# Three attentions with heads of 8: twenty direct heads over six PSUM banks, and another form of the DMAs that build the stacks

## The chip, the cores and the metric

The kernel runs on one core of a Trainium2 chip (trn2). The metric is the time of one execution on the device in microseconds (us). TensorE is called PE, VectorE DVE, ScalarE ACT, GpSimd POOL, and SyncE, which only issues DMAs here, SP.

## The reference, cut to what matters

A decoder of four layers on `x` of 8 x 256 tokens x 128 features, all float32. Three of its twelve blocks are attentions with 16 heads of 8 features each: the one at the head of layer 1's hybrid block, layer 1's attention to the context, and layer 3's attention to the context. All three have this core (this is layer 3's, 8 batches of 256 queries and 256 keys):

```
q = (query @ Wq.T + bq).reshape(b, tq, 16, 8).transpose(0, 2, 1, 3)
k = (key @ Wk.T + bk).reshape(b, tk, 16, 8).transpose(0, 2, 1, 3)
v = (value @ Wv.T + bv).reshape(b, tk, 16, 8).transpose(0, 2, 1, 3)
scores = jnp.einsum('bhqd,bhkd->bhqk', q, k) / np.sqrt(8)
attn = jax.nn.softmax(scores, axis=-1)
out = jnp.einsum('bhqk,bhkd->bhqd', attn, v)
```

Layer 1's attention to the context has no projections of queries and keys. The rest of the decoder (wide attentions, gated and routed MLPs, a state-space block, scans) is not touched.

## The kernel before, in words

The program is one sequence of blocks. The class `Narrow` writes all three attentions; each has 8 x 16 = 128 heads, numbered g = 16 b + h, taken in pairs, one pair to a step p. The orders of PE, DVE and ACT are written out by hand in loops over p from -24 to 71.

A head is used twice. In **comparing** (`weigh_and_compare_pe`, the `compares` part) PE computes its scores with queries on the partitions (two halves of 128 x 256, one PSUM bank) and DVE reduces them to the negated maximum of each query (`maximum_dve`, L1256). When a batch's 16 maxima are there, `cut_maxima_dve` (L1271 to L1279) cuts them into three bf16 parts and PE transposes them (L1240, `neg`). In **weighing**, ten steps behind (`AHEAD = 10`), PE adds the maxima (selector products, `SEL`) and the scores the other way round, ACT takes the exponential (L1342), and PE sums the values (`sum_pe`). So comparing pair x = 2 (p + 10) stands in the same step as weighing pair p: x = 16 and 18 are compared at p = -2 and -1, and at p = 0 weighing begins beside the comparing of x = 20.

Scores must be exact to float32, but PE is fast only in bf16. So queries and keys are cut into three bf16 parts by POOL (`cut_pool`, L1403 to L1419; four steps a batch), and eight products of parts are stacked into 8 x 8 = 64 partitions for one head. The stacks are made through DRAM: `spread` (L1446) writes the parts to `parts`, and L1465 reads a batch's stack of 128 partitions x 2 x 4096 bytes, 1 MB, back. A write is 64 partitions x 3 (or 2) copies x 512 bytes, and a batch has 12 of them. All go out on SP's queue in `sync`, batch after batch, except the eight of batch 1's first two parts, which ACT issues in `act` after its masks. Per batch `sync` waits for the batch's writes (`parts_out`), then issues the read; from batch 3 on the read also waits until the buffer's old heads are scored (there are three stacks), which is at step p = 8 (b - 2) - 1. The batch is first needed at x = 16 b, which is p = 8 (b - 2) + 6.

Before the first stack is there, the first 16 heads (`DIRECT = 16`) are compared **directly** in float32: ACT makes a masked copy of the queries for each pair (L1382) and PE multiplies it with all keys, two heads of a pair on the two halves of the array's rows. Banks 4 and 5 hold the scores of one head each, alternately; before a head's products PE waits for the maximum of the head that had the bank (`maxed`). Banks 0 to 3 are those of weighing, 6 and 7 serve sums and all small work.

```
        direct = x < self.DIRECT
        if compares and (x == self.DIRECT or x % H == 0 and not direct):
            pe.wait_ge(*s.loaded_stack(x // H % 3).at(x // H))
```

Of the kernel before, what the change touches and what calls it, by code (L numbers as in the profile page):

```python
# [10 lines left out]
AXX = mybir.AxisListType.X  # L11


B, S, D = 8, 256, 128
P = 128
# [3 lines left out]
H = 16  # L19
HD = D // H  # L20
HW = 64
# [259 lines left out]
def table_act(k, act, func):  # L281

    k.tables += 1
    act.activation(k.small[:, k.tables:k.tables + 1], k.small[:, 0:1], func)
# [183 lines left out]
def mm(pe, out, lhsT, rhs, start=True, stop=True):  # L468
    return pe.matmul(out, lhsT, rhs, start=start, stop=stop, skip_group_check=True)  # L469
# [592 lines left out]
class Narrow:  # L1062
# [6 lines left out]


    AHEAD = 10
    DIRECT = 16
    FIRST = -24
    STEPS = B * H // 2
    LAST = STEPS + 8
# [41 lines left out]
    def masked(self, b, w):  # L1117
        if b == 0:
            return self.expo[w // 2][:, w % 2 * S:(w % 2 + 1) * S]
        return self.expo[7][:, w * S:(w + 1) * S] if w < 2 else self.accs[w - 2]  # L1120

    def other(self, p):

        r, i = divmod(p, H // 2)
        kind, b = (("project", r + 3), ("value", r + 1), ("turn 0", r - 1), ("turn 1", r - 1), (None, 0), ("back", r - 1),
                   ("neg", r + 1), ("out", r - 1))[i]
        there = kind is not None and 0 <= b < B
        if there and self.projection is None and kind in ("project", "value"):
            there = False
        return (kind, b) if there else None  # L1130
# [14 lines left out]
    def weigh_and_compare_pe(self, pe, p):  # L1145
        k, s = self.k, self.k.s
        weighs, compares = 0 <= p < self.STEPS, 0 <= p + self.AHEAD < self.STEPS
        a, x = 2 * p, 2 * (p + self.AHEAD)
        if weighs:
            b, h = divmod(a, H)  # L1150
            if h == 0:
                pe.wait_ge(*s.flip_s.at("neg", b))
            if a == 0:
                pe.wait_ge(*s.loaded_stack(0).at(0))
            for i in range(2):
                g, rows = a + i, slice(HW * i, HW * (i + 1))
                if g >= 4:
                    pe.wait_ge(*s.weighed.at("e", g - 4))
                mm(pe, k.bank[g % 4][:, :], k.SEL[rows, h + i, :], self.negt[b % 3][rows, :].unsqueeze(1).to_broadcast([HW, HALVES, S]), True, False)
# [3 lines that stand above are left out]
        if compares and direct:  # L1163
            pe.wait_ge(*s.lowered.at("masked", x // H, x % H // 2))
        for i in range(2):
            g, y = a + i, x + 1 - i
            if compares and y - 2 >= 0:
                pe.wait_ge(*s.maxed.at("x", y - 2))
            for c in range(HALVES):
                if weighs:  # L1170
                    m = mm(pe, k.bank[g % 4][:, c * S:(c + 1) * S], self.head(1, g)[:, c * P:(c + 1) * P], self.head(0, g), False, True)
                    if c:
                        m.then_inc(*s.scored.up("s", g))
                if compares:
                    queries, keys = self.head(0, y), self.head(1, y)
                    if direct:
                        rows = slice(HW * (y % 2), HW * (y % 2 + 1))
                        queries, keys = self.masked(y // H, y % H // 2)[rows, :], self.sources(y // H)[1][rows, :]
                    m = mm(pe, k.bank[4 + i][:, c * S:(c + 1) * S], queries[:, c * P:(c + 1) * P], keys)
                    if c:  # L1180
                        m.then_inc(*s.compared.up("x", y))

# [69 lines left out]
    def maximum_dve(self, dve, g):  # L1252
        s, (b, h) = self.k.s, divmod(g, H)
        neg = self.neg[b % 2].rearrange("p (t h) -> p t h", h=H)
        dve.wait_ge(*s.compared.at("x", g))
        dve.tensor_reduce(neg[:, :, h], self.k.bank[5 - g % 2][:, :].rearrange("p (t s) -> p t s", s=S), AXX, ALU.max,  # L1256
                          negate=True).then_inc(*s.maxed.up("x", g))

    def cut_maxima_dve(self, dve, b):
# [74 lines left out]
    def act(self, act):  # L1334
        k, s = self.k, self.k.s
        for p in range(self.FIRST, self.LAST):
# [12 lines left out]
            kind, b = self.other(p) or (None, 0)  # L1349
            if kind == "project":  # L1350
# [3 lines left out]
                if b == 3:  # L1354
                    act.wait_ge(*s.compared.at("x", self.DIRECT - 2))
                for n in range(2):
# [12 lines left out]
                act.activation(self.negt[b % 3], k.bank[7][:, :].bitcast(BF16)[:, 0:S], ACT.Copy).then_inc(*s.flip_s.up(kind, b))  # L1369
            if p in (self.FIRST, self.FIRST + H // 2):  # L1370
                self.mask_act(act, (p - self.FIRST) // (H // 2))
            if p == self.FIRST + H // 2:
                for c in range(2):
                    self.spread(act, 1, c)

    def mask_act(self, act, b):

        s, queries = self.k.s, self.sources(b)[0]
        if self.projection is not None:
            act.wait_ge(*s.stacked.at("project", b))  # L1380
        for w in range((min(self.DIRECT, (b + 1) * H) - b * H) // 2):
            act.activation(self.masked(b, w), queries, ACT.Identity, scale=self.k.w["same_d"][:, w:w + 1]).then_inc(*s.lowered.up("masked", b, w))  # L1382
# [53 lines left out]
    def spread(self, e, b, c):  # L1436

        s, dram, wide = self.k.s, self.k.parts_dram[b % 2], H // 2 * S
        e.wait_ge(*s.pool.at("cut", b, (0, 2, 3)[c]))
        for n, parts in enumerate((QUERY_PARTS, KEY_PARTS)):  # L1440
            among = [j for j in range(HD) if parts[j] == c]
            for o in range(2):
                row = n * P + o * HW + among[0] * HD
                place = bass.AP(dram.tensor, dram.offset + row * wide, [[S, HW], [(among[1] - among[0]) * HD * wide, len(among)], [1, S]])
                part = self.part(b, c)[o * HW:(o + 1) * HW, n * S:(n + 1) * S].unsqueeze(1).to_broadcast([HW, len(among), S])
                e.dma_start(place, part).then_inc(*s.parts_out[b % 2].up(*((b,) if (c, n, o) == (2, 1, 1) else (b, c, n, o))))  # L1446

    def sync(self, sp):


        k, s, wide = self.k, self.k.s, H // 2 * S
        for b in range(B):
            dram = k.parts_dram[b % 2]
            if b >= 2:
                sp.wait_ge(*s.loaded_stack((b - 2) % 3).at(b - 2))
            if b != 1:
                for c in range(3):
                    self.spread(sp, b, c)
            if b == 0:
                for c in range(2, 3):  # L1460
                    self.spread(sp, 1, c)
            if b >= 3:
                sp.wait_ge(*s.scored.at("s", (b - 2) * H - 1))
            sp.wait_ge(*s.parts_out[b % 2].at(b))
            sp.dma_start(self.stacks[b % 3].rearrange("p (n x) -> p n x", n=2),  # L1465
                         bass.AP(dram.tensor, dram.offset, [[wide, P], [P * wide, 2], [1, wide]])).then_inc(*s.loaded_stack(b % 3).up(b))


def raw_attention(k):
# [2957 lines left out]
```

## Time and profile before

| | us |
|---|---|
| median of 3 runs (2190.21 to 2195.07) | 2190.42 |
| the profiled execution, its own time | 2180.52 |
| its span in the profile | 2178.7 |
| first attention, first direct product to first weighing product | 348.25 to 372.06 |
| second attention, the same | 976.49 to 1004.24 |
| third attention, the same | 1904.35 to 1930.91 |

PE is busy for 87% of the span, DVE 70%, ACT 60%, POOL 27%. The profile is of one execution; times in its views count from the start of the span. An instruction's line is that of `kernel.py` before.

### The profile page before, as it was taken

Reading aid. Unit: us, or ns where it says so; the run is one execution under the profiler, and the core shown is the slowest. Engines: PE = TensorE matmul, PEld = TensorE weight load, DVE = VectorE, ACT = ScalarE, POOL = GpSimd, SP = SyncE. Lnnn points to the kernel's source line nnn. Section 1 sums busy time; section 2 is a strip of 40 time slices with the busy share of each in tenths; the row PEclk is TensorE's granted clock in tenths of the full one; section 3 lists DMA queues with packets and bytes.
Section 4 is the critical chain, followed back from the end, with each engine's and each line's share of the span. In section 5 each row is a group of like instructions: output and inputs, shape, how many; then the busy total and the mean of one; then the engine's idle time right before and its main releaser. Section 6 shows DMA issues by size and latency. Waiting matters only on the chain.

```text
span 2178.7 us, 37918 instructions
## 1 busy us (share of the span) xinstructions
PE 1892.0 (87%) x13392; PEld 1272.6 (58%) x13392; DVE 1522.0 (70%) x3631; ACT 1308.5 (60%) x2797; POOL 588.9 (27%) x569
## 2 busy tenths in 40 slices
PE   7999777997999999968987488999997997789896
PEld 5777565445777777644444255566665676544465
DVE  5777677865777677557847847989997457568553
ACT  5777533775878888734765746667665222347632
POOL 3223003102544443414101003344343001031035
PEclk9999897998999999977988699999999899889998
DMA  4000004411000000015402000000000100264022
GB/s 202 2 2 2 1 1 124 133 56 39 1 2 1 1 1 1 1 28 159 126 1 80 0 1 1 1 1 1 1 1 1 58 2 1 85 187 137 17 60 88
DMA packets 80155, 87.39 MB, mean 40 GB/s; under 512 B 6578, under 2 KB 70115, under 8 KB 79073
## 3 DMA queue, kind: packets, MB, share of 16 engines
q1 hardware_dynamic: 73633, 80.12, 11.6%
q10 hardware_dynamic: 4992, 2.36, 0.4%
q0 software_dynamic: 1344, 2.49, 0.4%
q8 instruction: 109, 1.79, 0.3%
q14 instruction: 77, 0.63, 0.1%
HBM read 54.39 MB, written 30.70 MB: 39 GB/s over the span
## 4 chain that ended last, share of the span: by engine, by line
PE 55%; DVE 28%; ACT 8%; issue 6%; POOL 2%; DMA 1%; ACTq 0%; DVEq 0%; POOLq 0%; SPq 0%
PE bank L469 46%; DVE scratch L1256 5%; PE bank L653 2%; ACT XN L2053 2%; PE bank L3010 2%; DVE scratch L3128 2%; DVE scratch L3148 2%; PE bank L368 2%; PE bank L693 1%; DVE XN L3168 1%; DVE stats L245 1%; DVE scratch L1665 1%; DVE w_keep L1952 1%; ACT L2131 1%; PE bank L1225 1%
## 5 line engine op out<-in xcount | busy, mean ns | idle before, releaser
L469 PE MATMUL bank<-scratch 64*128 64x256 bf16 (+5 forms) x2960 | 314.5, 303 | 22.2 <-DVE scratch L1256 13.3
L1256 DVE TENSOR_REDUCE scratch<-bank 128x2 f32<-128x512 f32 x384 | 244.5, 686 | 66.9 <-PE bank L469 66.1
L469 PE MATMUL bank<-w_keep,scratch 128*128 128x128 f32 (+4 forms) x1760 | 244.4, 330 | 18.7 <-DVE scratch L1995 4.1
L469 PEld LDWEIGHTS bank<-scratch 64*128 64x128 bf16 (+3 forms) x2960 | 178.8, 123 | 130.7 <-DVE scratch L1256 50.6
L1342 ACT ACTIVATE w_keep<-bank 128x512 f32<-128x512 f32 x384 | 212.5, 597 | 53.1 <-PE bank L469 45.2
L469 PE MATMUL bank<-XNT,w_keep 128*128 128x256 f32 (+4 forms) x800 | 235.6, 434 | 6.2 <-POOL w_keep L2192 5.7
L469 PEld LDWEIGHTS bank<-w_keep,scratch 128*128 128x128 f32 (+3 forms) x1760 | 182.9, 185 | 83.4 <-issue 54.9
L469 PEld LDWEIGHTS bank<-XNT,w_keep 128*128 128x128 f32 x800 | 149.1, 196 | 56.9 <-issue 28.3
L469 PE MATMUL bank<-w_early,scratch 64*128 64x256 f32 (+3 forms) x1152 | 160.9, 342 | 17.6 <-ACT w_early L3228 8.7
L469 PE MATMUL bank<-w_keep 128*32 128x256 f32 (+2 forms) x1728 | 153.4, 394 | 19.3 <-ACT w_keep L1342 5.4
L469 PEld LDWEIGHTS bank<-w_early,scratch 64*128 64x128 f32 (+3 forms) x1152 | 117.1, 182 | 62.6 <-issue 21.7
L795 ACT ACTIVATE scratch<-bank,scratch 128x256 f32<-128x256 f32 x256 | 100.3, 475 | 54.9 <-DVE scratch L721 54.9
L469 PE MATMUL bank<-scratch,w_early 128*128 128x256 f32 (+2 forms) x416 | 122.3, 438 | 8.5 <-DVE scratch L2555 4.4
L3228 ACT ACTIVATE w_early<-bank,scratch 128x256 f32<-128x256 f32 x172 | 82.9, 562 | 72.6 <-DVE scratch L3132 72.6
L721 DVE TENSOR_REDUCE scratch<-bank 128x2 f32<-128x512 f32 x128 | 82.5, 686 | 61.7 <-PE bank L469 61.6
L469 PEld LDWEIGHTS bank<-w_keep 128*32 128x32 f32 (+2 forms) x1728 | 70.2, 121 | 88.0 <-issue 47.2
L469 PE MATMUL bank<-XNT,w_early 128*128 128x256 f32 (+1 forms) x384 | 115.4, 430 | 4.5 <-ACT XNT L383 1.6
L3337 POOL TENSOR_TENSOR w_early<-w_early,scratch 128x1024 f32<-128x1024 f32 x43 | 81.4, 1892 | 136.6 <-DVE scratch L3153 136.6
L368 PE MATMUL bank<-w_keep,XN 128*128 128x128 f32 x192 | 48.2, 426 | 79.0 <-DVE XN L318 76.1
L3128 DVE TENSOR_REDUCE scratch<-bank 128x2 f32<-128x512 f32 x128 | 87.5, 684 | 22.1 <-PE bank L469 22.1
L469 PEld LDWEIGHTS bank<-scratch,w_early 128*128 128x128 f32 x416 | 72.1, 199 | 47.9 <-issue 30.1
L1952 DVE SCALAR_TENSOR_TENSOR w_keep<-w_keep,w_early 128x256 f32<-128x256 f32 x192 | 98.5, 562 | 0.1
(460 smaller groups left out, 3843.3 us busy)
## 6 DMA issues: line engine op xcount, KB each, us to landing
scratch<-parts SPq DMA_DIRECT2D x24, 1024.0 KB, 5.0
parts<-scratch SPq DMA_DIRECT2D x168, 96.0 KB, 2.3
parts<-scratch SPq DMA_DIRECT2D x96, 64.0 KB, 2.1
w_early<-pack_l3f SPq DMA_DIRECT2D x1, 5206.0 KB, 17.3
parts<-scratch ACTq DMA_DIRECT2D x24, 96.0 KB, 2.9
w_keep<-pack_l2f SPq DMA_DIRECT2D x1, 2124.0 KB, 13.1
w_early<-pack_mamba SPq DMA_DIRECT2D x1, 2120.0 KB, 18.9
w_keep<-pack_l2x SPq DMA_DIRECT2D x1, 2049.0 KB, 8.5
```

Of the source, the lines that this page charges most:

```text
L368: t = pe.transpose(k.bank[q][:, j * P:(j + 1) * P], src(i), k.w["ident"])
L469: return pe.matmul(out, lhsT, rhs, start=start, stop=stop, skip_group_check=True)
L653: m = pe.transpose(self.k.bank[3 + o][:, c * S + t * P:c * S + (t + 1) * P], self.expo[g % 4][:, t * S + c * P:t * S + (c + 1) * P], self. ...
L721: dve.tensor_reduce(self.neg[g % 4], self.scores(g)[:, :].rearrange("p (t s) -> p t s", s=S), AXX, ALU.max, negate=True).then_inc(*s.maxed ...
L795: a = act.activation(self.expo[g % 4][:, t * S:(t + 1) * S], self.scores(g)[:, t * S:(t + 1) * S], ACT.Exp, bias=self.neg[g % 4][:, t:t + 1])
L1256: dve.tensor_reduce(neg[:, :, h], self.k.bank[5 - g % 2][:, :].rearrange("p (t s) -> p t s", s=S), AXX, ALU.max, negate=True).then_inc(*s. ...
L1342: act.activation(self.expo[g % 8], k.bank[g % 4][:, :], ACT.Exp, scale=HD ** -0.5).then_inc(*s.weighed.up("e", g))
L1952: o = dve.scalar_tensor_tensor(out=yv[:, j, :], in0=xv[:, j, tap:tap + S], scalar=scale, in1=yv[:, j, :], op0=ALU.mult, op1=ALU.add)
L2053: a = act.activation(self.by_head(self.early[u % 2])[:, t, h, :], self.upto, ACT.Copy, scale=a3[:, t, h:h + 1])
L3128: dve.tensor_reduce(neg, self.k.bank[o][:, :].rearrange("p (t s) -> p t s", s=S), AXX, ALU.max, negate=True).then_inc(*s.maxed.up("x", p, o))
L3228: a = act.activation(self.weights(p, o)[:, t * S:(t + 1) * S], self.k.bank[o][:, t * S:(t + 1) * S], ACT.Exp, bias=self.bias[p % 2][:, o * ...
L3337: pool.tensor_tensor(ex, ex, self.sums[p % 2].unsqueeze(2).to_broadcast([P, 2 * HALVES, S]), ALU.mult).then_inc(*s.pool.up("scaled", p))
```

## The change

Three things, in all three attentions.

- `DIRECT` goes from 16 to 20, so two more pairs (x = 16 and 18, of batch 1) are compared in float32 and the wait for stack 1 moves from x = 16 (p = -2) to x = 20 (p = 0). ACT makes two more masked copies.
- The scores of the first 16 heads go around six banks, 4, 5, 0, 1, 2, 3 (`compare_bank`), and PE waits for the maximum of the head six places before (`reused`) instead of two. From head 16 on it is banks 4 and 5 as before. For banks 0 to 3 PE also waits until they are emptied of the transposes ahead of the attention (`turned_at`).
- `spread` writes 128 features at once, six writes a batch instead of twelve, with another order of rows in `parts`; ACT issues none any more. SP's order at the start is now batch 0's six, batch 1's first two, stack 0's read, batch 1's other four, stack 1's read. A read is four DMAs of 64 partitions x 4096 bytes instead of one of 128 x 2 x 4096, and its address list in DRAM begins with a count of 8 (8 x 8 rows) instead of 128.

```
-    DIRECT = 16
+    DIRECT = 20
...
+    def compare_bank(self, y):
+        m = y ^ 1
+        return self.k.bank[(4, 5, 0, 1, 2, 3)[m % 6] if m < H else 4 + m % 2]
+    def reused(self, y):
+        m = y ^ 1
+        m -= 6 if m < H else 2
+        return m ^ 1
...
-            if compares and y - 2 >= 0:
-                pe.wait_ge(*s.maxed.at("x", y - 2))
+            if compares and self.reused(y) >= 0:
+                pe.wait_ge(*s.maxed.at("x", self.reused(y)))
+            if compares and 2 <= y ^ 1 < 6:
+                pe.wait_ge(*self.turned_at((y ^ 1) - 2))
...
-            if p == self.FIRST + H // 2:
-                for c in range(2):
-                    self.spread(act, 1, c)
...
-            for o in range(2):
-                row = n * P + o * HW + among[0] * HD
-                place = bass.AP(dram.tensor, dram.offset + row * wide, [[S, HW], [(among[1] - among[0]) * HD * wide, len(among)], [1, S]])
-                part = self.part(b, c)[o * HW:(o + 1) * HW, n * S:(n + 1) * S].unsqueeze(1).to_broadcast([HW, len(among), S])
-                e.dma_start(place, part).then_inc(*s.parts_out[b % 2].up(*((b,) if (c, n, o) == (2, 1, 1) else (b, c, n, o))))
+            place = bass.AP(dram.tensor, dram.offset + (n * P + among[0] * H) * wide, [[S, P], [(among[1] - among[0]) * H * wide, len(among)], [1, S]])
+            part = self.part(b, c)[:, n * S:(n + 1) * S].unsqueeze(1).to_broadcast([P, len(among), S])
+            e.dma_start(place, part).then_inc(*s.parts_out[b % 2].up(*((b,) if (c, n) == (2, 1) else (b, c, n))))
...
-            sp.dma_start(self.stacks[b % 3].rearrange("p (n x) -> p n x", n=2),
-                         bass.AP(dram.tensor, dram.offset, [[wide, P], [P * wide, 2], [1, wide]])).then_inc(*s.loaded_stack(b % 3).up(b))
+            for o in range(2):
+                for n in range(2):
+                    rows = bass.AP(dram.tensor, dram.offset + (n * P + o * HD) * wide, [[H * wide, HD], [wide, HD], [1, wide]])
+                    sp.dma_start(self.stacks[b % 3][o * HW:(o + 1) * HW, n * wide:(n + 1) * wide], rows).then_inc(
+                        *s.loaded_stack(b % 3).up(*((b,) if o and n else (b, o, n))))
```

On SP, at the start of the first attention, the order was this (a batch's stack is the `scratch<-parts` row, shapes are partitions x copies or halves x elements):

```order
L1446 DMA parts<-scratch 64x3x256 x8
L1446 DMA parts<-scratch 64x2x256 x8
L1465 DMA scratch<-parts 128x2x2048 x2
L1446 DMA parts<-scratch 64x3x256 x8
L1446 DMA parts<-scratch 64x2x256 x4
L1465 DMA scratch<-parts 128x2x2048
```

And now it is this:

```order
L1454 DMA parts<-scratch 128x3x256 x4
L1454 DMA parts<-scratch 128x2x256 x2
L1454 DMA parts<-scratch 128x3x256 x2
L1474 DMA scratch<-parts 64x1x2048 x4
L1454 DMA parts<-scratch 128x3x256 x2
L1454 DMA parts<-scratch 128x2x256 x2
L1474 DMA scratch<-parts 64x1x2048 x4
```

Stack 0's read moved ahead of four of batch 1's writes, stack 1's read stands behind them, and each read is now four DMAs.

On PE, from the thirteenth head of the first attention on (`w_keep` are the masked queries and the direct keys, `scratch` the stacks), the order was:

```order
L469 MATMUL bank4<-w_keep 128x256 x2
L469 MATMUL bank5<-w_keep 128x256 x2
L469 MATMUL bank4<-w_keep 128x256 x2
L469 MATMUL bank5<-w_keep 128x256 x2
L469 MATMUL bank4<-scratch 128x256 x2
L469 MATMUL bank5<-scratch 128x256 x2
L1240 MATMUL bank7<-IDB,scratch 128x128 x2
L469 MATMUL bank4<-scratch 128x256 x2
L469 MATMUL bank5<-scratch 128x256 x2
L469 MATMUL bank0<-scratch,SEL 128x512
```

And now:

```order
L469 MATMUL bank4<-w_keep 128x256 x2
L469 MATMUL bank5<-w_keep 128x256 x2
L469 MATMUL bank0<-w_keep 128x256 x2
L469 MATMUL bank1<-w_keep 128x256 x2
L469 MATMUL bank4<-scratch,w_keep 128x256 x2
L469 MATMUL bank5<-scratch,w_keep 128x256 x2
L1253 MATMUL bank7<-IDB,scratch 128x128 x2
L469 MATMUL bank4<-scratch,w_keep 128x256 x2
L469 MATMUL bank5<-scratch,w_keep 128x256 x2
L469 MATMUL bank0<-scratch,SEL 128x512
```

The places of the instructions are the same; the last four direct heads of batch 0 go to four banks instead of two, and the two pairs around the transposes (L1240, now L1253) are direct products in float32 instead of products of the stack.

## Rows read from the trace of the kernel before

**Rows 1.** The page, costliest groups: the reductions of comparing (count, busy us, mean ns)

```profile
L1256 DVE TENSOR_REDUCE scratch<-bank 128x2 f32<-128x512 f32 x384 | 244.5, 686 | 66.9 <-PE bank L469 66.1
```

**Rows 2.** Timeline, second attention: start us, us, engine line operation xcount [idle before <-releaser]

```profile
973.46 1.15 POOL L1419 TENSOR_TENSOR scratch<-scratch 128x512 bf16<-128x512 f32 x1
...
976.49 2.08 PE L469 MATMUL bank<-CT,w_keep 64*128 64x256 f32 x8 [2.69 <-ACT w_keep L1382]
...
991.09 2.58 PE L469 MATMUL bank<-CT,w_keep 64*128 64x256 f32 x8 [0.34 <-DVE scratch L1256]
...
994.01 2.58 PE L469 MATMUL bank<-CT,w_keep 64*128 64x256 f32 x8 [0.34 <-DVE scratch L1256]
...
1004.24 1.20 PE L469 MATMUL bank<-scratch 64*128 64x256 bf16 x8
...
1014.06 0.90 PE L469 MATMUL bank<-scratch 64*128 64x256 bf16 x8 [0.47 <-DVE scratch L1256]
```

**Rows 3.** Timeline, first attention

```profile
350.25 1.28 DVE L1256 TENSOR_REDUCE scratch<-bank 128x2 f32<-128x512 f32 x2
...
350.32 1.16 POOL L1419 TENSOR_TENSOR scratch<-w_keep,scratch 128x512 bf16<-128x512 f32 x1
...
368.60 0.71 PE L469 MATMUL bank<-scratch 64*128 64x256 bf16 x4 [0.52 <-DMA scratch<-parts]
...
372.06 1.20 PE L469 MATMUL bank<-scratch 64*128 64x256 bf16 x8
...
383.86 0.90 PE L469 MATMUL bank<-scratch 64*128 64x256 bf16 x8 [0.47 <-DVE scratch L1256]
...
385.37 3.72 DVE L1256 TENSOR_REDUCE scratch<-bank 128x2 f32<-128x512 f32 x6
```

**Rows 4.** Timeline, third attention

```profile
1915.12 0.71 PE L469 MATMUL bank<-w_keep,CT 128*128 128x128 f32 x4 [3.03 <-ACT scratch L1357]
...
1930.91 1.20 PE L469 MATMUL bank<-scratch 64*128 64x256 bf16 x8
```

**Rows 5.** Timeline of SP's queue: start us, us for all issues together, xcount

```profile
2.12 0.43 SPq L4212 DMA_DIRECT2D w_early<-pack_l  x1
...
359.37 2.02 SPq L1465 DMA_DIRECT2D scratch<-parts  x2
...
971.38 10.62 SPq L1446 DMA_DIRECT2D parts<-scratch  x16
...
1031.54 0.36 SPq L1465 DMA_DIRECT2D scratch<-parts  x1
...
1045.91 0.37 SPq L1465 DMA_DIRECT2D scratch<-parts  x1
...
1894.10 0.35 SPq L4272 DMA_DIRECT2D w_early<-pack_l3f  x1
...
1916.26 1.73 SPq L1465 DMA_DIRECT2D scratch<-parts  x2
```

**Rows 6.** The page, DMA issues: xcount, KB each, median us from issue to landing

```profile
scratch<-parts SPq DMA_DIRECT2D x24, 1024.0 KB, 5.0
parts<-scratch SPq DMA_DIRECT2D x168, 96.0 KB, 2.3
...
w_early<-pack_l3f SPq DMA_DIRECT2D x1, 5206.0 KB, 17.3
```

**Rows 7.** Windows: stretch, us, busy time (xcount) of each engine, PE clock, DMA share, GB/s

```profile
370.00:374.00 4.00, 3.71 (x18) 1.64 (x19) 3.70 (x7) 1.52 (x3) 0.00 (x0) 0.50 0.52 127
...
450.00:453.50 3.50, 3.50 (x46) 1.59 (x40) 3.29 (x8) 2.70 (x6) 0.00 (x0) 1.00 0.84 298
...
450.50:453.00 2.50, 2.50 (x34) 1.23 (x28) 2.30 (x4) 2.14 (x5) 0.00 (x0) 1.00 0.90 369
...
1700.00:1710.00 10.00, 10.00 (x24) 5.12 (x24) 5.33 (x15) 3.06 (x5) 0.00 (x0) 0.78 0.07 21
...
985.00:990.00 5.00, 4.41 (x15) 3.49 (x16) 1.99 (x4) 0.00 (x0) 5.00 (x5) 0.50 0.97 371
```

More of the change, by code:

```diff
@@ L1178, in weigh_and_compare_pe @@
                         queries, keys = self.masked(y // H, y % H // 2)[rows, :], self.sources(y // H)[1][rows, :]
-                    m = mm(pe, k.bank[4 + i][:, c * S:(c + 1) * S], queries[:, c * P:(c + 1) * P], keys)
+                    m = mm(pe, self.compare_bank(y)[:, c * S:(c + 1) * S], queries[:, c * P:(c + 1) * P], keys)
                     if c:
@@ L1255, in maximum_dve @@
         dve.wait_ge(*s.compared.at("x", g))
-        dve.tensor_reduce(neg[:, :, h], self.k.bank[5 - g % 2][:, :].rearrange("p (t s) -> p t s", s=S), AXX, ALU.max,
+        dve.tensor_reduce(neg[:, :, h], self.compare_bank(g)[:, :].rearrange("p (t s) -> p t s", s=S), AXX, ALU.max,
                           negate=True).then_inc(*s.maxed.up("x", g))
@@ L1455, in sync @@
                 sp.wait_ge(*s.loaded_stack((b - 2) % 3).at(b - 2))
-            if b != 1:
-                for c in range(3):
-                    self.spread(sp, b, c)
+            for c in range(b == 1, 3):
+                self.spread(sp, b, c)
             if b == 0:
-                for c in range(2, 3):
-                    self.spread(sp, 1, c)
+                self.spread(sp, 1, 0)
             if b >= 3:
```

## The prediction, made before the changed kernel had run

> **What bounds the kernel now.** I read the page first. PE is busy for most of the span, but the change touches 384 of DVE's reductions and the products before them, and of those reductions DVE stood idle 66.9 us in all, nearly all of it waiting for PE [rows 1]. So I looked at where that idle time lies. The timeline puts it at the three starts. In the second attention the direct pairs follow each other every 994.01 - 991.09 = 2.92 us [rows 2], while six reductions in a row take 3.72 us, 1.24 a pair [rows 3]: with two banks PE and DVE take turns. The bound of that start is this ping-pong: 27.75 us from the first direct product (976.49) to the first weighing product (1004.24) [rows 2], with PE at the lower of its two clock levels, 1.2 GHz (granted clock 0.50 [rows 7]).
>
> The first attention is different. Its pair x = 16 waited last for a DMA, the read of stack 1 at 368.60 [rows 3]. The DMA engines are close to full there. So two chains run side by side up to the first weighing: PE and DVE, and cut, write, read, cut, write, read. In the first attention the DMAs end last, in the second the compute. In the third, PE also stood 3.03 us because ACT, busy with issuing DMAs, emptied a bank late, until 1915.12 [rows 4]. After the start each batch takes 1045.91 - 1031.54 = 14.4 us [rows 5], and no read is waited for.
>
> **The compute chain, after.** With six banks a pair needs no turn of DVE's. The two heads run side by side as the first pair did: 2.08 us at the lower clock at 976.49 [rows 2]. Ten pairs then take at most 20.8 us, or, if the clock rises, 20 reductions of 0.62 = 12.4 us. Two more direct pairs are in that count; ACT's two more masks hide in its idle time. In the second attention this makes PE ready for weighing between 976.49 + 2.08 + 12.4 = 991 and 976.49 + 20.8 = 997.3, against 1004.2. In the first, DVE starts at 350.25 [rows 3]; 12.4 us, and an estimated 3.5 for the cut of the maxima and the projections in between, give 366, that is 18 us after its first product. In the third the same 18 us from 1904.35 give 1922, the stall of 3.03 us gone since ACT issues nothing.
>
> **The DMA chain, after.** PE's first weighing step now waits for stack 1, so this chain decides. Its terms:
>
> - Issue. Twelve-write batches cost 10.62 / 16 = 0.66 us a DMA [rows 5]. DMAs of 128 partitions cost 0.43, as at 2.12 [rows 5]. I take 0.45 for a write. A read's piece has 64 partitions, so 0.65: four take 2.6 us.
> - Writes' data. With only writes in flight, 127 GB/s at a DMA share of 0.52 [rows 7]: 1.05 MB takes 8.26 x 0.52 = 4.3 us of all 16 engines. Batch 1's last four writes are 10/16 of it, 2.7 us.
> - Reads' data. 1.05 MB at 298 GB/s and share 0.84 is 2.95 us of all engines, at 369 and 0.90 it is 2.56 [rows 7]; 2.75 in the middle. Issue to landing is 5.0 [rows 6].
> - How many engines a piece uses. From 1700 to 1710 one DMA was in flight, L4263, whose list begins with 127 rows: a DMA share of 0.07 and 21 GB/s [rows 7], one engine of sixteen. Lists that begin with 128 or 64 fill all of them. A count is shared out in equal parts or not at all, so I read a list that begins with 8 as **eight engines**. Data then take 5.5 us instead of 2.75, and a read lands 7.75 us after its first issue. The bounds are 5.0 (sixteen engines) and 5.0 + 3 x 2.75 = 13.25 (four).
>
> The Trainium skill, page "DMA: Bandwidth & Descriptors", section "Why a DMA increments its semaphore by 16 and not by 1", says that a DMA spreads over the largest number up to 16 which divides the slowest dimension of both its access patterns; here that is 8, of 8 and 64. By it the sum is the one below, and without it the one of the first rival. The same page's "Rules for kernel authors" speaks against the pieces in themselves: two transfers to disjoint halves of the partitions only serialize, so one of 128 is as good. No row of this case shows such a pair.
>
> The pieces all go to the same eight engines, and batch 1's four writes, issued behind them on the same queue, are done on those only after the read's data. So from stack 0's first issue, r0: read 7.75, writes 2.7, read 7.75: **stack 1 lands at r0 + 18.2**, and weighing starts 0.1 later. Stack 2 follows stack 1's issue (r0 + 10.45) by 7.75 + 4.3 + 7.75 = 19.8.
>
> First attention. The last cut ends at 350.32 + 1.16 = 351.48 [rows 3]; two writes, the second from 352.0, land 2.3 [rows 6] + 0.4 (twice the bytes) later: r0 = 354.7, where it was 359.37 [rows 5]. Weighing at 354.7 + 18.3 = 373.0 against 372.06: 0.9 lost. Stack 2 lands at 365.15 + 19.8 = 384.95; its pair was at 383.86 [rows 3] and would be at 384.8: **1.1 lost** in all.
>
> Second. The last cut ends at 974.61 [rows 2], r0 = 977.8. Weighing at 996.1 (inside PE's 991 to 997) against 1004.24: 8.1 gained. Stack 2 lands at 988.25 + 19.8 = 1008.05, and its pair was at 1014.06 [rows 2]: **6.0 gained**, 2 given back.
>
> Third. The writes queue behind pack_l3f, which lands at 1894.10 + 17.3 = 1911.4 [rows 5, 6]. 4.3 us of writes behind it end at 1915.7 at the latest; before, with ACT's among them, the read was issued at 1916.26 [rows 5]. I take r0 = 1915.5. Weighing at 1933.8 against 1930.91 [rows 4]: **2.9 lost**. Stack 2 comes with its pair.
>
> Later batches. A read may start at p = 8 (b - 2) - 1 and is needed at + 6, six steps and a bit of eight in 14.4 us: 10.8 us. 7.75 fits, so nothing is lost there. SP's queue itself gets shorter, 6 x 0.45 + 4 x 0.65 = 5.3 us a batch instead of 12 x 0.66 + 0.36 = 8.3; that was covered and is worth nothing.
>
> Sum: 6.0 - 1.1 - 2.9 = **2 us gained** on the profiled execution's 2180.5. The median of the runs is 9.9 above that execution, and the difference is carried over: 2190.4 - 2 = 2188. Own range of this case: each start is uncertain by about 1 us in the reads (2.56 to 2.95) and more in the writes, if they overlap with the reads better than in sequence (up to 2.7 us in each start); r0 of the third by 2.5. That makes 10 us faster to 3 slower, 2180 to 2193.
>
> **Rivals.**
>
> 1. *Sixteen engines all the same.* A read lands at 5.0, its issues hiding behind data; batch 1's writes are issued at r0 + 2.6 to 4.4 and land at 7.1; stack 1 at r0 + 12.1. First: 366.9, 5.2 gained. Second: PE decides, 991 to 997, about 9.5 gained. Third: 1927.7, 3.2 gained. Sum 18, so 2172. For it: both sides together have 64 rows, and the hardware might count those. Against it: the row of one engine at 21 GB/s.
> 2. *Slower: reads late in every batch.* If a piece is spread over four engines or fewer, a read takes 13.25 us, over the 10.8 that a batch leaves. That decides from 10.8 on, and then it is paid five times in each attention, (13.25 - 10.8) x 15 = 37 us. Each start loses two longer reads, 11 us, 33 in all. 2190 - 2 + 70 = 2258. For it: one engine for 127 rows shows that a count can cost most of the engines. Against it: 8 has no reason to fall to 4.
> 3. *The change doesn't do what its banks promise*: PE stays at the lower clock (0.50 at 88% busy [rows 7]) and ten pairs of 2.08 end at 997.3. With eight engines stack 2 decides anyway, so it costs nothing in my sum; with sixteen it takes some 3 us from rival 1. It has no price of its own.
>
> **How the numbers follow.** A measurement of this kernel can tell 0.3% from no change, 6.6 us. Eight engines: 0.75, of which 0.13 faster by more (the writes overlap), 0.53 within, 0.09 slower by more (the third start loses more, or the first weighing stays at the lower clock for longer). Sixteen: 0.17, faster. Four or fewer: 0.08, slower. Faster 0.30, same 0.53, slower 0.17. The likeliest is 2188. The range reaches down to rival 1 and up to the main case's end, 2171 to 2193; beyond it are rival 2 and the main case's tails.
>
> **What would show it.** In the changed profile: pieces of 256 KB that together land 7 to 8 us after the first issue (5 by rival 1, 13 by rival 2); the first weighing product released by the DMA of a stack in all three starts; DVE's idle time before its reductions falling from 66.9 us by some 15 in the direct pairs and coming back as one wait of several us before the 21st; the third start longer than 26.6 us, the second shorter than 27.75 by 5 or more. The prediction is wrong if PE is never seen waiting for a stack, or if PE waits for one in the later batches.

## The result, and the profile after

The changed kernel takes **2196.45 us** (median of 20 runs, 2191.35 to 2202.18), the kernel before 2190.45 (20 runs, 2188.34 to 2198.54): ratio **1.0024**, 95% interval 1.0015 to 1.0032, some 5 to 6 us slower. The forecast was 2188, range 2171 to 2193: the time lies above the range and on the other side, though within the 0.3% that I had called "same". The profiled execution spans 2189.3 us; before 2178.7.

The costliest groups of the page of the changed kernel (count | busy us, mean ns | idle before, and what ended it), then its DMA issues (count, KB each, median us to landing):

```profile
L469 PE MATMUL bank<-scratch 64*128 64x256 bf16 (+6 forms) x2936 | 308.1, 303 | 43.2 <-DMA scratch<-parts 24.2
L1269 DVE TENSOR_REDUCE scratch<-bank 128x2 f32<-128x512 f32 x384 | 243.0, 685 | 68.1 <-PE bank L469 67.5
...
scratch<-parts SPq DMA_DIRECT2D x96, 256.0 KB
parts<-scratch SPq DMA_DIRECT2D x96, 192.0 KB, 3.6
parts<-scratch SPq DMA_DIRECT2D x48, 128.0 KB, 5.2
```

DVE's idle time before its reductions, which the six banks were to remove, is 68.1 us and was 66.9 [rows 1]. Beside it stands what was nearly absent before: of PE's idle time before the products of stacks, 24.2 us ended with the DMA of a stack.

Where they lie, the PE part of the timeline shows (start us, us, operation, [idle before <-releaser]), in the first, second and third attention:

```profile
353.13 3.83 PE L469 MATMUL bank<-w_keep 64*128 64x256 f32 x32
...
373.05 1.03 PE L469 MATMUL bank<-scratch 64*128 64x256 bf16 x8 [6.97 <-DMA scratch<-parts]
...
977.07 9.85 PE L469 MATMUL bank<-CT,w_keep 64*128 64x256 f32 x64 [2.69 <-ACT w_keep L1392]
...
998.15 1.03 PE L469 MATMUL bank<-scratch 64*128 64x256 bf16 x8 [1.79 <-DMA scratch<-parts]
...
1010.88 0.61 PE L469 MATMUL bank<-scratch 64*128 64x256 bf16 x8 [3.56 <-DMA scratch<-parts]
...
1930.43 1.03 PE L469 MATMUL bank<-scratch 64*128 64x256 bf16 x8 [10.30 <-DMA scratch<-parts]
```

The ping-pong is gone: 64 direct products (eight pairs) take 9.85 us, 1.23 a pair, where a pair came every 2.92 us [rows 2]. In all three starts PE is then done early and waits for stack 1: 6.97, 1.79 and 10.30 us. For stack 2 it waits once more in each: 1.08 us (its pair starts at 385.16), 3.56 and 0.51. These six waits are the 24.2 us.

SP's queue in the same three starts (start us, us of all issues together, count):

```profile
347.02 5.10 SPq L1454 DMA_DIRECT2D parts<-scratch  x8
352.60 2.59 SPq L1474 DMA_DIRECT2D scratch<-parts  x4
355.24 2.67 SPq L1454 DMA_DIRECT2D parts<-scratch  x4
364.10 2.46 SPq L1474 DMA_DIRECT2D scratch<-parts  x4
...
449.89 2.46 SPq L1474 DMA_DIRECT2D scratch<-parts  x4
...
971.98 5.29 SPq L1454 DMA_DIRECT2D parts<-scratch  x8
977.72 2.46 SPq L1474 DMA_DIRECT2D scratch<-parts  x4
980.23 2.47 SPq L1454 DMA_DIRECT2D parts<-scratch  x4
988.43 2.46 SPq L1474 DMA_DIRECT2D scratch<-parts  x4
...
1001.02 2.46 SPq L1474 DMA_DIRECT2D scratch<-parts  x4
...
1901.05 6.22 SPq L1454 DMA_DIRECT2D parts<-scratch  x8
1909.42 2.51 SPq L1474 DMA_DIRECT2D scratch<-parts  x4
...
1920.50 3.28 SPq L1474 DMA_DIRECT2D scratch<-parts  x4
```

From stack 0's read to the first weighing it is 373.05 - 352.60 = **20.45 us**, 998.15 - 977.72 = 20.43, and 1930.43 - 1909.42 = 21.01. The forecast had 18.3. Of the first attention's 20.45, 11.5 pass until stack 1's read may be issued (its batch's last writes are done) and 8.95 are that read.

**A measure for each attention.** From the first write on SP's queue to the first issue of the last read is a stretch that holds the start and nearly all batches of the attention. Before, the first attention had 448.90 - 348.43 = 100.47 us; after, 449.89 - 347.02 = 102.87. The table gives it for every kernel of this study, as difference to before:

| kernel | first | second | third | sum | ratio to before, timed |
|---|---|---|---|---|---|
| before | 100.47 us | 103.28 us | 105.05 us | | |
| changed | +2.4 | -2.8 | +3.1 | +2.7 | 1.0024 |
| e1 | -1.5 | -9.3 | -5.5 | -16.3 | 0.9921 |
| e12 (e1 again) | -1.5 | -9.0 | -2.8 | -13.4 | 0.9936 |
| e2 | +6.0 | -0.1 | +7.4 | +13.4 | 1.0064 |
| e3 | -1.8 | -8.9 | -2.0 | -12.8 | 0.9928 |
| e4 | -3.9 | -8.9 | -5.3 | -18.1 | 0.9913 |
| e5 | -1.1 | -10.0 | -5.2 | -16.2 | 0.9945 |
| e10 | -0.7 | -10.2 | -5.2 | -16.1 | 0.9939 |
| e6 | +3.7 | +0.3 | +0.1 | +4.1 | 1.0032 |
| e7 | +3.8 | +0.9 | +0.2 | +4.9 | 1.0024 |
| e9 | +7.5 | -0.4 | +3.6 | +10.7 | 1.0058 |
| e8 | -0.5 | -8.7 | -3.5 | -12.7 | 0.9955 |
| e11 | +2.7 | -8.2 | -1.8 | -7.3 | 0.9981 |

The sum agrees with the timed difference within some 4 us. It is one execution each, and e1 and e12, the same kernel, differ by 2.7 us in the third attention; so nothing hangs here on a difference under 3 us in one start.

**Why the spans differ by 10.6.** Behind the third attention, where the change touches nothing, the profiled execution after has a hole. The first row is before, the second after (DVE's row of the same operation):

```profile
2123.81 0.42 DVE L3907 TENSOR_TENSOR w_keep<-bank,w_early 128x256 f32<-128x256 f32 x1 [4.40 <-PE bank L469]
```

```profile
2136.04 0.42 DVE L3916 TENSOR_TENSOR w_keep<-bank,w_early 128x256 f32<-128x256 f32 x1 [16.41 <-remote]
```

The profiled executions of e1 to e4 have it too, those of e5 to e12 do not, and the median of the kernel before was 2191.4 beside the former and 2179.4 and 2179.3 beside the latter. And e12 is e1 once more: the same kernel has the hole in one set of runs (15.09 us) and not in the other. So it goes with the chip or the hour, not with the kernel, and ratios to the runs beside them are what can be compared. The profile does not name its cause, and I did not try for it. It is also the likely reason why the profiled execution of before lay 9.9 under its median.

### The profile page after: what moved, and what is told of

It reads as the page before. It is cut to its first block, busy times and chain, and to the rows that moved or that the text cites. A ratio compares the mean times of both kernels' runs of the same rounds, so it can differ in the third digit from the quotient of the medians.

```text
span 2189.3 us, 37904 instructions
## 1 busy us (share of the span) xinstructions
PE 1878.7 (86%) x13416; PEld 1268.1 (58%) x13416; DVE 1527.1 (70%) x3631; ACT 1311.5 (60%) x2803; POOL 590.5 (27%) x569
## 3 DMA queue, kind: packets, MB, share of 16 engines
q8 instruction: 109, 1.79, 0.3%
## 4 chain that ended last, share of the span: by engine, by line
PE 29%; DVE 17%; issue 3%; ACT 2%; DMA 2%; POOL 1%; SPq 1%; POOLq 0%; DVEq 0%; ACTq 0%
PE bank L469 25%; DVE scratch L1269 3%; PE bank L3019 2%; DVE scratch L3137 2%; DVE scratch L3157 2%; DVE XN L3177 1%; PE bank L368 1%; POOL w_early L3346 1%; DMA parts<-scratch 1%; DMA scratch<-parts 1%; DVE w_early L2569 1%; DVE scratch L3148 1%; PE bank L1238 1%; DVE stats L245 1%; DVE scratch L3141 0%
## 5 line engine op out<-in xcount | busy, mean ns | idle before, releaser
L469 PE MATMUL bank<-scratch 64*128 64x256 bf16 (+6 forms) x2936 | 308.1, 303 | 43.2 <-DMA scratch<-parts 24.2
L1269 DVE TENSOR_REDUCE scratch<-bank 128x2 f32<-128x512 f32 x384 | 243.0, 685 | 68.1 <-PE bank L469 67.5
L469 PEld LDWEIGHTS bank<-scratch 64*128 64x128 bf16 (+4 forms) x2936 | 178.2, 123 | 147.6 <-DVE scratch L1269 43.5
L469 PE MATMUL bank<-w_keep 128*32 128x256 f32 (+2 forms) x1728 | 140.9, 388 | 14.2 <-ACT w_keep L1355 5.4
L469 PEld LDWEIGHTS bank<-w_keep 128*32 128x32 f32 (+2 forms) x1728 | 63.8, 118 | 76.9 <-issue 39.0
## 6 DMA issues: line engine op xcount, KB each, us to landing
w_early<-pack_mamba SPq DMA_DIRECT2D x1, 2120.0 KB, 18.6
```

Of the source, the lines that this page charges most:

```text
L1269: dve.tensor_reduce(neg[:, :, h], self.compare_bank(g)[:, :].rearrange("p (t s) -> p t s", s=S), AXX, ALU.max, negate=True).then_inc(*s.ma ...
```

## The experiments

Theory 1: the banks do what they promise, but the pieces of the reads run on eight DMA engines, each read is longer for it, and the starts now wait for them. Rival: the banks or the four more direct heads are worth little, and the reads' form does not matter. All ratios are to the kernel before, timed beside the run.

### The two halves of the change apart: e1 and e2

e1 is the kernel before with the six banks and 20 direct heads; all DMAs stay:

```
-    DIRECT = 16
+    DIRECT = 20
...
+    def compare_bank(self, y):
+        m = y ^ 1
+        return self.k.bank[(4, 5, 0, 1, 2, 3)[m % 6] if m < H else 4 + m % 2]
```

> Only the six banks and 20 direct heads, with the DMAs of before (twelve writes a batch, eight of batch 1 on ACT, one read of 128 partitions). Theory 1, the reads on eight engines ate the gain: stack 1 lands when it did, about 368.6, 991 and 1925 us in the three attentions, and weighing starts right then or when PE is ready, so 3, 9 and 6 us are gained, 2190 - 18 = 2172. Theory 2, the two more float32 pairs and the banks cost what they save: within 3 us of 2190.

Measured: 2179.31 us against 2191.43, ratio **0.9921** (0.9899 to 0.9944). Theory 1's sign and most of its size: 12 us by the medians, 17 by the ratio, for 18. PE waits for stack 1 in none of the three starts there, and only once for a later stack, 0.72 us in the third.

e2 is the other half: writes of 128 features, reads in four pieces, everything on SP's queue, two banks and 16 direct heads as before:

```
-            for o in range(2):
-                row = n * P + o * HW + among[0] * HD
...
+            place = bass.AP(dram.tensor, dram.offset + (n * P + among[0] * H) * wide, [[S, P], [(among[1] - among[0]) * H * wide, len(among)], [1, S]])
...
+            for o in range(2):
+                for n in range(2):
+                    rows = bass.AP(dram.tensor, dram.offset + (n * P + o * HD) * wide, [[H * wide, HD], [wide, HD], [1, wide]])
```

> Only the other DMAs (six writes of 128 features, reads in four pieces, all on SP), with two banks and 16 direct heads. Theory 1: x = 16 at p = -2 waits for stack 1, which lands about 26 us after the first write of each attention, so weighing starts about 3.5 us after that: first attention 4 to 5 us later than in the kernel before, third 6 to 8 later, second unchanged or 1 later. 2190 + 12 = 2202. Theory 2 (the DMAs are harmless, something in the compute lost it): 2190 within 3.

Measured: 2208.35, ratio **1.0064** (1.0041 to 1.0088). By the medians the banks are worth 2191.43 - 2179.31 = 12 us and the new DMAs cost 2208.35 - 2191.43 = 17; by the ratios it is 17 and 14. So the DMAs eat the gain.

That the medians sum to +5, the whole change, is luck. By the ratios the sum is -3, and start by start (table) the halves do not add up. In the second attention e1 has -9.3 and e2 -0.1, but both together -2.8: with two banks the ping-pong ends last there and hides the slower DMAs, and with six banks they cost 9.3 - 2.8 = 6.5 us. In the first attention it is the other way round: +6.0 by themselves, 2.4 + 1.5 = 3.9 with the banks.

### What of the DMAs: e3 and e4

e3 is the changed kernel with one line other, the list of each piece. It takes the rows in another order than the stack wants, so e3 and e4 do not compute the attention's result; instructions, shapes and waits are those of the changed kernel.

```
-    rows = bass.AP(dram.tensor, dram.offset + (n * P + o * HD) * wide, [[H * wide, HD], [wide, HD], [1, wide]])
+    rows = bass.AP(dram.tensor, dram.offset + (n * P + o * HW) * wide, [[wide, HW], [1, wide]])
```

> The changed kernel, but each piece of a read takes 64 rows that follow each other in DRAM, so that its list begins with 64; same bytes, same number of DMAs, but the rows of the stack come in another order, so the later scores are those of other features. Theory 1: a read lands about 5 to 5.5 us after its first issue instead of 8.8, stack 1 some 7 us earlier; 5, 9 and 3 us gained against before, so about 2172 to 2175. Theory 2 (order of the queue, ACT relieved of its writes, not the number of engines): within 3 us of 2196.

Measured: 2177.86, ratio **0.9928** (0.9909 to 0.9948). The same number of DMAs, the same bytes and the same waits, and 2196.45 - 2177.86 = 18.6 us are gone; by the ratios it is 0.96%, 21 us. Its start (SP's queue, and PE's first weighing):

```profile
351.25 3.28 SPq L1474 DMA_DIRECT2D scratch<-parts  x4
354.58 2.36 SPq L1454 DMA_DIRECT2D parts<-scratch  x4
360.48 2.37 SPq L1474 DMA_DIRECT2D scratch<-parts  x4
...
367.71 1.03 PE L469 MATMUL bank<-scratch 64*128 64x256 bf16 x8 [2.96 <-DMA scratch<-parts]
```

From r0, stack 0's first issue, to the weighing 367.71 - 351.25 = 16.5 us, where the changed kernel has 20.45; the DMA share of e3's last read, alone from 446 to 449, is 0.94. Stack 1's read now takes 7.2 us instead of 8.95, and comes 9.2 after stack 0's instead of 11.5.

e4 goes on from there, one DMA for a read:

```
+            sp.dma_start(self.stacks[b % 3].rearrange("p (n x) -> p n x", n=2),
+                         bass.AP(dram.tensor, dram.offset, [[wide, P], [P * wide, 2], [1, wide]])).then_inc(*s.loaded_stack(b % 3).up(b))
```

> The changed kernel, but a batch's read is one DMA of 128 partitions x 2 again (rows in another order than the stack wants, as in e3_reads_16). Theory 1: the pieces in themselves cost little beside the number of engines; one issue of 0.4 us instead of 2.5 lets batch 1's writes go 2 us earlier: 2170 to 2173, 1 to 2 us under e3_reads_16. If the pieces are what costs, it is far under e3_reads_16.

Measured: 2175.07, ratio **0.9913** (0.9893 to 0.9934). Its two reads stand 361.98 - 353.72 = 8.3 us apart:

```profile
353.72 0.36 SPq L1471 DMA_DIRECT2D scratch<-parts  x1
354.12 3.38 SPq L1454 DMA_DIRECT2D parts<-scratch  x4
361.98 0.36 SPq L1471 DMA_DIRECT2D scratch<-parts  x1
```

So with reads on sixteen engines the change is worth 16 to 19 us by the ratios (18 by rival 1), as much as the banks alone (e1, 0.9921): the new writes and their place on SP's queue cost nothing that shows.

### Banks without the four direct heads: e5, e10, e12

e5 is e1 with `DIRECT = 16`, e10 with 18, e12 is e1 once more.

> The kernel before with the six banks alone: 16 direct heads and all DMAs as before. If the ping-pong of the two banks was the price of the starts (theory 1), the second attention gains its 8 to 9 us and the third its 3 us, while the first still waits for stack 1 and gains nothing: 2178 to 2181, no different from e1_banks_direct (2179.3), and the four more direct heads are worth nothing. Rival: the four heads carry half of what e1 gained, because the pair 16 of every start waits for stack 1's read: then 2185, and the trace shows that pair released by a stack's DMA in the second attention too.

Measured: 2167.65 against 2179.4, ratio **0.9945** (0.9931 to 0.9959). The trace shows what theory 1 had not said: the first pair from a stack waits in every start, as the rival had it for the second.

```profile
365.45 0.40 PE L469 MATMUL bank<-scratch 64*128 64x256 bf16 x4 [2.46 <-DMA scratch<-parts]
...
990.81 0.61 PE L469 MATMUL bank<-scratch 64*128 64x256 bf16 x4 [4.19 <-DMA scratch<-parts]
...
1914.41 0.39 PE L469 MATMUL bank<-scratch 64*128 64x256 bf16 x4 [2.29 <-DMA scratch<-parts]
```

> e5_banks_16 with 18 direct heads. In e5_banks_16 the first pair from the stacks waited 2.46 us, 4.19 us and 2.29 us for stack 1 in the three starts; in e1_banks_direct (20) that wait was gone, but the direct products came later. One pair more covers about 2.1 us at the lower clock, so 18 should hide half of the wait: 1 to 3 us under e5_banks_16, ratio to before 0.993 to 0.994. Rival: it is a matter of one wait against another and the ratio stays 0.9945.

> e1_banks_direct once more, beside e10_banks_18: whether 20, 18 or 16 direct heads (0.9945) make a difference. Theory: no, all three within 0.002 of each other, ratio 0.9925 to 0.9945. Rival: 20 heads are better by what the wait for stack 1 took in e5_banks_16 (2 to 4 us in each start), 0.990 to 0.992.

Measured: e10 2165.98, ratio **0.9939** (0.9922 to 0.9957); e12 2165.50, ratio **0.9936** (0.9918 to 0.9954), both beside 2179.3. The three intervals overlap almost wholly: 16, 18 or 20 direct heads are not told apart. The four heads hide a wait for stack 1 and take about as long themselves. The banks alone carry the gain.

### The number of engines by itself: e6, e7, e9

These three are the kernel before with nothing but the read cut into the same four pieces (64 rows of 4 KB each), so that data and writes are as before. e6 writes a piece's list as 64 rows, e7 as 8 by 8 of the same rows. From e6 to e7:

```
-    rows = bass.AP(dram.tensor, dram.offset + (n * P + o * HW) * wide, [[wide, HW], [1, wide]])
+    rows = bass.AP(dram.tensor, dram.offset + (n * P + o * HW) * wide, [[HD * wide, HD], [wide, HD], [1, wide]])
```

> The kernel before with each stack's read in four pieces whose lists begin with 64 rows. If the number of engines is what the pieces cost (theory 1), a read takes 6.2 us here from its first issue (as in e3_reads_16) instead of 5.0: two of them stand before the first attention's first weighing, 2.4 us, one in the third's, 1 us, none in the second's, where PE and DVE end last: 2193 to 2195. Rival, issue: every DMA more on the queue costs by itself, and this kernel is as slow as e7_before_eight, both near 2200.

> The kernel before with each read in the same four pieces of the same rows, but the lists written as 8 by 8 rows: the same bytes, the same issues, another first number alone. Theory 1: eight engines, reads of 8.8 us (8.1 to 10.2) from first issue to landing, 2.6 more than in e6_before_pieces; twice in the first start, about 5 us, and once in the third, 2 to 3 us: 2200 to 2203, 7 us above e6_before_pieces. Rival: the first number of the list doesn't matter, both kernels within 2 us, and the slow reads of the changed kernel come from its writes of 128 features.

Measured: e6 2186.56, ratio **1.0032** (1.0020 to 1.0044); e7 2185.23, ratio **1.0024** (1.0014 to 1.0034). No difference, which is what both rivals expected, though neither kernel is near the 2200 of e6's rival. But e7 had not made eight engines at all: in a stretch with only a read in flight its engines are all busy.

```profile
454.00:457.00 3.00, 3.00 (x40) 1.41 (x36) 2.81 (x6) 2.29 (x6) 0.00 (x0) 1.00 1.01 240
```

(Windows of e7: us, the five engines' busy time, PE clock, DMA share 1.01, 240 GB/s.) Eight times eight rows that lie behind each other are 64 rows. That the list was merged to one of 64 is inferred from the share; where it is merged is not shown. So e7 says nothing on eight engines. So e9 leaves a blank row behind every eight in DRAM, in the writes and in the read:

```
-                row = n * P + o * HW + among[0] * HD
+                row = ((n * 2 + o) * HD + among[0]) * (HD + 1)
...
+    rows = bass.AP(dram.tensor, dram.offset + (n * 2 + o) * HD * (HD + 1) * wide, [[(HD + 1) * wide, HD], [wide, HD], [1, wide]])
```

> e7_before_eight showed pieces 1.2 us apart, as e6_before_pieces: since its rows lay behind each other, its 8 by 8 list was the same as one of 64, and its first number decided nothing. Here a blank stretch of one row lies behind every eight rows in DRAM, so that the 8 by 8 stays; all else is e7_before_eight. Theory 1 (eight engines): pieces land together 8 to 10 us after the first issue instead of 6.2; stack 1 of the first attention comes 4 to 6 us later than in e6_before_pieces, the third start 2 to 3 us longer, the second unchanged: 0.3% to 0.45% above e6_before_pieces, that is a ratio to before of 1.006 to 1.008. Rival (the list's form doesn't matter, the writes of 128 features slow the reads): ratio 1.003 as in e6_before_pieces, and pieces 1.2 us apart.

Measured: 2190.19 against 2179.3, ratio **1.0058** (1.0038 to 1.0079), just under what theory 1 expected (1.006 to 1.008). Its interval and e6's overlap by 0.0006. Against e7, which differs from it by the gap alone, they do not meet (1.0038 and 1.0034), though the two were timed in different sets of runs. Three traces side by side: windows with only a read in flight, of the changed kernel, of e9 and of e6, each in its own fence.

```profile
453.00:457.00 4.00, 4.00 (x49) 2.20 (x46) 3.42 (x8) 2.62 (x6) 0.00 (x0) 1.00 0.50 176
```

```profile
456.00:460.00 4.00, 4.00 (x50) 2.06 (x48) 3.31 (x6) 2.94 (x6) 0.00 (x0) 1.00 0.51 181
```

```profile
453.00:457.00 4.00, 4.00 (x56) 2.01 (x56) 3.81 (x9) 3.29 (x7) 0.00 (x0) 1.00 1.01 232
```

A DMA share of 0.50 and 0.51 is eight engines' worth of sixteen. The Trainium skill's rule (page "DMA: Bandwidth & Descriptors", section "Why a DMA increments its semaphore by 16 and not by 1") is the largest number up to 16 that divides the slowest dimension of both lists, here 8, and these two traces agree. With e7 they agree only if the list counts as merged, not as it was written. The waits of the first pair from a stack, e9 and then e6 (first and third attention):

```profile
373.55 0.61 PE L469 MATMUL bank<-scratch 64*128 64x256 bf16 x4 [6.99 <-DMA scratch<-parts]
...
1937.22 0.61 PE L469 MATMUL bank<-scratch 64*128 64x256 bf16 x4 [4.85 <-DMA scratch<-parts]
```

```profile
372.31 0.61 PE L469 MATMUL bank<-scratch 64*128 64x256 bf16 x4 [5.20 <-DMA scratch<-parts]
...
1933.62 0.61 PE L469 MATMUL bank<-scratch 64*128 64x256 bf16 x4 [1.11 <-DMA scratch<-parts]
```

Eight engines lengthen the first start by 7.5 - 3.7 = 3.8 us over e6 and the third by 3.5; the second not, since there PE and DVE end last in this kernel (table). In the changed kernel, whose computing is quicker, nothing covers them any more, and the same cause costs 16 to 21.

### Who issues: e8 and e11

e8 is e1, e11 is e5, with ACT issuing only the first part of the second batch:

```
-                for c in range(2):
-                    self.spread(act, 1, c)
+                self.spread(act, 1, 0)
...
-                for c in range(2, 3):
+                for c in range(1, 3):
```

> e1_banks_direct with ACT issuing only the first part of the starts' second batch, SP the other two: ACT's queue loses 2.6 us of issues in each start, SP's gains them. If what is left of the starts in e1_banks_direct is the DMA chain (stack 1 and 2 late), SP's longer list delays it by up to 2.6 us in the first attention and the time rises to 2181 to 2184; if ACT's issues still hold PE's banks there, the time falls to 2174 to 2177. I take the first as a little likelier.

> e8_act_half with 16 direct heads. There stack 1 comes 2 to 3 us later than in e5_banks_16 (SP issues more before it), and with 16 direct heads nothing covers it: 5 to 8 us above e5_banks_16 over the three starts, ratio to before 0.997 to 0.998. Rival (the wait for stack 1 is worth nothing since the clock or stack 2 decides behind it): 0.9945 to 0.9955.

Measured: e8 2167.94, ratio **0.9955** (0.9940 to 0.9969), not told apart from e12. e11 2176.07, ratio **0.9981** (0.9969 to 0.9993), 8.4 us above e5 and just past the end of what was expected (5 to 8 us, 0.998). Its waits for stack 1 are 5.4, 2.5 and 6.4 us longer than e5's. The read goes out later behind SP's first write than in e5, for the four writes more before it, by 3.7, 2.6 and 2.4 us; the rest of the longer waits was not located.

```profile
370.37 0.61 PE L469 MATMUL bank<-scratch 64*128 64x256 bf16 x4 [7.89 <-DMA scratch<-parts]
...
997.70 0.61 PE L469 MATMUL bank<-scratch 64*128 64x256 bf16 x4 [6.64 <-DMA scratch<-parts]
...
1921.92 0.61 PE L469 MATMUL bank<-scratch 64*128 64x256 bf16 x4 [8.68 <-DMA scratch<-parts]
```

With 20 direct heads (e8) most of the same delay is hidden; its interval and e11's just touch at 0.9969. This is where the direct heads earn something: as cover for a later stack.

## Why the prediction was wrong

**Right: what takes over.** The chain that decides is the one of DMAs, cut, write, read, with PE ready before it in all three starts. The ping-pong went as written (1.23 us a pair, DVE's 1.24), and DVE's idle time came back as waits around the 21st reduction, 7.28 us in the first start and 10.61 in the third: 68.1 us in all for 66.9. PE was ready within the bounds in the first start (its selector products at 365.46 against 366).

**Right: eight engines**, with the share of 0.50 as the row that proves it, and so is rival 1's size: with sixteen (e3, ratio 0.9928) the gain is 15.8 us, where 18 were worked out. Rival 2 did not come: no read is late in the later batches, whose pace in the first attention is 15.47 us (reads at 434.42 and 449.89) where it was 15.49 before (433.41 and 448.90). Rival 3, the low clock, was seen (0.81 for the stretch from 977 to 987, 0.50 while PE waited); as PE then waited for stacks in all three starts, nothing shows that it decided anything.

**The step that failed: "a read lands 7.75 us after its first issue".** The term was 2.75 us of all engines' data doubled, behind 2.25 of latency. The rate was a little high: 1.05 MB at 176 GB/s is 6.0 us, not 5.5. More came from what I had put in sequence and priced as if each ran alone: stack 1's read took 8.95 us in the first start, 998.15 - 988.43 = 9.7 in the second and 1930.43 - 1920.50 = 9.9 in the third. In all three the next batch's writes are issued 2.6 to 3.4 us after the read begins, and while both are in flight the DMA share is 1.10 (992.40 to 994.40), so all sixteen engines are busy, the read's eight among them. But the writes explain only a part. The last read of each attention has no write behind it; it is issued at 449.89, 1072.44 and 2009.24, and its engines are done by 458.0, just before 1081.6, and by 2017.8, as the DMA share at the end of these rows shows:

```profile
458.00:460.00 2.00, 1.93 (x30) 0.90 (x30) 1.75 (x5) 1.47 (x3) 0.00 (x0) 1.00 0.00 0
...
1081.00:1081.60 0.60, 0.60 (x14) 0.41 (x16) 0.60 (x2) 0.60 (x2) 0.00 (x0) 1.00 0.09 34
1081.60:1084.00 2.40, 2.33 (x30) 0.85 (x20) 2.02 (x4) 1.86 (x6) 0.00 (x0) 1.00 0.00 0
...
2017.80:2021.00 3.20, 2.83 (x34) 1.15 (x34) 3.13 (x7) 2.33 (x6) 0.00 (x0) 1.00 0.00 0
```

So a read on eight engines takes up to 8.1, 9.2 and 8.6 us even when it is alone. What is left for the writes is some 1 us of the 8.95 to 9.9, and what parts the three reads from each other is not shown. With stack 0's share, r0 to weighing is 20.4 to 21.0 for 18.3.

A second term was off and cost nothing: a write of 128 partitions was priced at 0.45 us of issue, from a single DMA, and took 0.67 (six in 4.00 us at 424.06). Nothing waited for it.

Start by start, as changes to before:

- *First.* Forecast 1.1 lost, measured 2.4 (table). r0 came 0.7 earlier than worked out (3.76 us after DVE's first reduction, which starts at 348.84, for 4.45) and the two reads 2.15 later.
- *Second.* Forecast 6.0 gained, measured 2.8. The first weighing is 998.15 - 971.98 = 26.17 us after the first write, where it was 1004.24 - 971.38 = 32.86 [rows 2, 5]: 6.7 gained of 8.1. Stack 2's pair comes at 1010.88 - 971.98 = 38.90 for 42.68 [rows 2, 5], 3.8 gained of 6.0, because stack 2 took 22.45 us from stack 1's issue, not 19.8. Another us goes behind it.
- *Third.* Forecast 2.9 lost, measured 3.1, by two errors that cancel: the writes behind pack_l3f were done sooner (r0 8.4 us after the first write; I had 11), and the reads took 2.7 longer.

The sum was to be 2 us gained; it is 2.7 lost in the trace and some 5 in the timed ratio. That is 5 to 8 us of error, of which the reads' length accounts for 2.1 to 2.7 us in each start. The other 2 to 3 us between the trace's sum and the timed ratio were not located.

**What the range missed.** It reached down to sixteen engines with a chance of 0.17, and up only to 3 us over the main case, on the ground that the one unknown, overlap of writes and reads, could only help. A length put together from a rate and a latency can miss upward as well: the rows it came from are of sixteen engines, and no row had a read on eight. Nor was there an overlap to read a price from: the DMA share of 0.97 from 985 to 990 [rows 7] is mostly two reads, issued from 982.05, with the next writes only from 987.77. A bound upward of the same size, 2.7 us in each start, on top of the others would have held the time.

**What is left of the change's idea.** The banks alone are worth 0.55% to 0.8%: e5, e10 and e12, at 2166 to 2168 us where before is at 2179, and e1, at 2179 where before is at 2191, are faster than both kernels, and they need no edit of a DMA.

## What to carry to other kernels

Two chains that end within a few microseconds of each other must be costed together: the gain of the one is only what the other leaves, and an edit that lengthens the second (here the reads' new row order, 19 to 21 us of the changed kernel, e3) can cost more than the first can give. When a layout changes a DMA's list, look at the first number of its merged form before anything else, and at the DMA share of a stretch where it runs alone: half a share is half the engines. And test the halves of a compound edit apart, but do not expect them to add up: here one was worth 12 to 17 us and the other cost 14 to 17, and the second attention hid the cost of the one until the other was there.

## What the runs showed that I had not expected

- A list of 8 by 8 rows that lie behind each other used all sixteen engines (share 1.01, e7), and with a gap of a row after each eight only eight (0.51, e9).
- Four pieces instead of one DMA cost by themselves, on sixteen engines: ratio 1.0032 (e6) and 1.0024 (e7), with 3.7 us of it in the first start, where two reads stand in a row. The Trainium skill, page "DMA: Bandwidth & Descriptors", section "Rules for kernel authors", has it that two transfers to disjoint halves of the partitions only serialize; these runs agree that nothing is gained, and the price is theirs. e3 against e4 (0.9928, 0.9913) points the same way, within the intervals.
- Small DVE operations of the cut took far longer than their size lets one think: 0.95, 0.64 and 1.02 us for operations on 128x64 and 128x32, beside casts of the first form that took 0.20. Each of the three ends 0.04 to 0.05 us after an operation of POOL on 128x512 ends (360.11, 360.78 and 362.06 below). The kernel before has one such cast too, 0.94 us at 1000.34, with POOL busy until 1001.22. That DVE waits there for POOL is argued from these ends; no run took POOL's work away. It drew out the cut to 3 us, and it was covered, as PE waited for stack 1 until 373.05.

```profile
358.95 1.16 POOL L1415 TENSOR_TENSOR scratch<-scratch 128x512 f32<-128x512 f32 x1
359.20 0.95 DVE L1284 CAST scratch<-scratch 128x64 bf16<-128x64 f32 x1
360.17 0.61 POOL L1427 CAST scratch<-scratch 128x512 bf16<-128x512 f32 x1
360.19 0.64 DVE L1286 TENSOR_TENSOR scratch<-scratch 128x32 f32<-128x32 f32 x1
360.86 0.20 DVE L1288 CAST scratch<-scratch 128x64 bf16<-128x64 f32 x1
360.86 1.20 POOL L1429 TENSOR_TENSOR scratch<-scratch 128x512 bf16<-128x512 f32 x1
361.09 1.02 DVE L1290 TENSOR_TENSOR scratch<-scratch 128x32 f32<-128x32 f32 x1
362.14 0.20 DVE L1292 CAST scratch<-scratch 128x64 bf16<-128x64 f32 x1
```
